# Long-convolution stage of an FFN block: filters split once into a rounded part and a remainder and loaded as two Toeplitz tiles in three slots

## The reference

```python
K = _get_kernel(log_dt, C, log_A_real, A_imag, Lq)          # (64, 1024)
y = jnp.fft.irfft(jnp.fft.rfft(u, n=n) * jnp.fft.rfft(K, n=n)[None], n=n)[..., :Lq]
y = (y + u * D[:, None]) * mask[:, None, :]
gate = qlinear(y, w_gate); up = qlinear(y, w_up)
h = jax.nn.silu(gate) * up
out = x + qlinear(h, w_down)
```

## Time and profile before

| what | value |
|---|---|
| timed runs | 1494.78 and 1500.71 us, median 1497.74 |
| span of the profiled execution, first to last instruction | 1487.8 us |
| TensorE matmul busy over the span | 1351.2 us (91%) |
| VectorE busy | 1002.7 us (67%) |
| ScalarE busy | 554.0 us (37%) |
| GpSimd busy | 489.5 us (33%) |
| moved by DMA | 139.21 MB, mean 94 GB/s |

### The profile page before, as it was taken

One profiled execution on the slowest core, in us unless ns is written; L12 is line 12 of the kernel. 1 busy time (PEld: TensorE's weight loads), 2 busy tenths in 40 slices (PEclk: granted clock), 3 DMA queues, 4 the chain that ended last, 5 costly groups with the idle time before them and its releaser, 6 DMA issues.

```text
span 1487.8 us, 23889 instructions
## 1 busy us (share of the span) xinstructions
PE 1351.2 (91%) x8030; PEld 810.5 (54%) x8126; DVE 1002.7 (67%) x1617; ACT 554.0 (37%) x882; POOL 489.5 (33%) x342
## 2 busy tenths in 40 slices
PE   2388888888899799999999999999999999999998
PEld 0377877778788444444444444444444444444443
DVE  7668788897998566665566556665566656665565
ACT  1155445555565133332333333332323323333333
POOL 2266666775777022112211212112221212112120
PEclk9999898999999899999999999999999999999999
DMA  0186677767785401211112111121112111121112
GB/s 4 28 254 209 214 228 221 226 204 226 247 265 172 140 15 36 57 49 35 35 42 56 42 35 35 49 56 35 35 35 63 42 35 35 49 55 37 35 29 71
DMA packets 44350, 139.21 MB, mean 94 GB/s; under 512 B 8396, under 2 KB 8606, under 8 KB 43038
## 3 DMA queue, kind: packets, MB, share of 16 engines
q1 hardware_dynamic: 44318, 138.79, 31.1%
HBM read 113.28 MB, written 25.49 MB: 93 GB/s over the span
## 4 chain that ended last, share of the span: by engine, by line
PE 51%; DVE 7%; issue 6%; ACT 1%; DVEq 0%; ACTq 0%
PE ps_o L1100 21%; PE ps_g L1074 14%; PE ps_u L1074 14%; DVE ps_o L1158 3%; PE ps_t L1085 3%; DVE h L1139 3%; DVE g_buf L1129 1%; ACT h_t L1207 1%; DVE res L1161 0%; DVEq L1138 0%; DVE h_max L1141 0%; DVE u_buf L1129 0%; ACT g_buf L1191 0%; DVEq L1157 0%; ACTq L1204 0%
## 5 line engine op out<-in xcount | busy, mean ns | idle before, releaser
L1236 POOL TENSOR_TENSOR h_int<-h,rounder 128x512 bf16<-128x512 f32 x186 | 186.7, 1025 | 778.7 <-ACT h L1197 778.7
L1074 PE MATMUL ps_g<-wgu,rows 128*128 128x512 bf16 (+1 forms) x1472 | 322.3, 358 | 8.2 <-PEq L377 4.9
L1074 PE MATMUL ps_u<-wgu,rows 128*128 128x512 bf16 (+1 forms) x1536 | 329.2, 357 | 0.0
L1129 DVE SCALAR_TENSOR_TENSOR g_buf<-ps_g,sx_all,wide 128x512 f32<-128x512 f32 x192 | 132.3, 689 | 286.8 <-PE ps_g L1074 286.6
L1191 ACT ACTIVATE g_buf<-g_buf 128x512 f32<-128x512 f32 x192 | 112.4, 585 | 569.9 <-DVE g_buf L1129 569.9
L1100 PE MATMUL ps_o<-wd,h_t 128*128 128x512 bf16 (+1 forms) x1376 | 312.2, 380 | 1.8 <-issue 0.2
L1100 PEld LDWEIGHTS ps_o<-wd,h_t 128*128 128x128 bf16 (+1 forms) x1408 | 134.2, 98 | 177.9 <-issue 34.4
L1074 PEld LDWEIGHTS ps_u<-wgu,rows 128*128 128x128 bf16 x1536 | 147.1, 98 | 151.6 <-issue 1.1
L1074 PEld LDWEIGHTS ps_g<-wgu,rows 128*128 128x128 bf16 x1536 | 140.0, 98 | 143.7 <-issue 13.2
L611 POOL TENSOR_TENSOR t_lo<-t_raw,t_hi 128x1024 fp32r<-128x1024 f32 x64 | 161.3, 2520 | 86.1 <-ACT t_hi L657 86.1
L1129 DVE SCALAR_TENSOR_TENSOR u_buf<-ps_u,sx_all,wide 128x512 f32<-128x512 f32 x192 | 132.6, 691 | 75.3 <-PE ps_u L1074 75.3
(11 more groups left out here) (148 smaller groups left out, 1225.3 us busy)
## 6 DMA issues: line engine op xcount, KB each, us to landing
t_raw<-k_rev SPq DMA_DIRECT2D x64, 512.0 KB, 6.1
rows<-in_x SPq DMA_DIRECT2D x64, 256.0 KB, 3.9
res<-in_x SPq DMA_DIRECT2D x64, 256.0 KB, 3.6
out_x<-res SPq DMA_DIRECT2D x64, 256.0 KB, 3.1
wide<-in_L_ffn_w_gate SPq DMA_DIRECT2D x22, 512.0 KB, 6.4
wide<-in_L_ffn_w_up SPq DMA_DIRECT2D x22, 512.0 KB, 7.3
wide<-in_L_ffn_w_down SPq DMA_DIRECT2D x8, 1376.0 KB, 6.6
xq_dram<-xq SPq DMA_DIRECT2D x32, 256.0 KB, 6.0
```

What stands on the lines that cost most here:

```text
L1074: last = pe.matmul(bank[:, 0:n], xq[:, par, c, :], wgu[:, NC - 1 - c, first + cols.start:first + cols.stop], start=(c == 0), stop=(c == NC ...
L1129: dve.scalar_tensor_tensor(out=buf[:, j % 2, 0:n], in0=bank[:, 0:n], scalar=sx, in1=s[:, cols], op0=ALU.mult, op1=ALU.mult).then_inc(gu_sc ...
L1236: pool.tensor_tensor(h_int[:, piece(j)], h[:, par, piece(j)], rounder[:].to_broadcast([P, n]), ALU.subtract).then_inc(h_int_ready, 1)
```

## The change

The filters are split in `long_filters`: ScalarE's copy out of PSUM writes the rounded part `k_hi`, VectorE subtracts it from PSUM into `k_lo`, and SP stores both, to `k_hi_rev` and `k_lo_rev` (two stores where there was one, each after its own semaphore). In stage 2 `t_raw`, `t_high` and `split_t` are gone; `load_t` is two loads of 512 KB, straight into `t_hi` and `t_lo`. The tiles have three slots: hh = 0 alternates between slots 0 and 1 by the parity of the iteration, hh = 1 always has slot 2. `load_t(i+2, 1)` waits for `conv_done` of `convolve(i+1, 1)`, `load_t(i+2, 0)` for that of `convolve(i, 0)`. The start of SP's list is in another order.

```diff
@@ long_filters, SP, VectorE, ScalarE
-            sp.dma_start(k_rev[:, L:L + P], zeros[:]).then_inc(k_stored, 16)
+            for k_rev in (k_hi_rev, k_lo_rev):
+                sp.dma_start(k_rev[:, L:L + P], zeros[:]).then_inc(k_stored, 16)
             for b in range(len(ps_k)):
-                sp.wait_ge(k_copied, b + 1)
                 first = b // 2 * HB
...
+                for done, k_rev, part in ((k_copied, k_hi_rev, k_hi), (k_split, k_lo_rev, k_lo)):
+                    sp.wait_ge(done, b + 1)
+                    heads = k_rev[2 * first + b % 2:2 * (first + HB):2, 0:L]
+                    sp.dma_start(heads.rearrange("a (q r) -> q a r", r=R),
+                                 part[:, b % 2, first:first + HB].bitcast(F32)).then_inc(k_stored, 16)
...
+            for b in range(len(ps_k)):
+                first = b // 2 * HB
+                dve.wait_ge(k_copied, b + 1)
+                dve.tensor_tensor(k_lo[:, b % 2, first:first + HB, :], ps_k[b][:],
+                                  k_hi[:, b % 2, first:first + HB, :].bitcast(F32), ALU.subtract).then_inc(k_split, 1)
...
-                act.activation(k_sb[:, b % 2, first:first + HB, :], ps_k[b][:], ACT.Copy).then_inc(k_copied, 1)
+                act.activation(k_hi[:, b % 2, first:first + HB, :], ps_k[b][:], ACT.Copy).then_inc(k_copied, 1)
@@ convolve_and_pack
-        t_raw = sb("t_raw", [P, 2, L])
-        t_hi = sb("t_hi", [P, 2, L], F32R)
-        t_lo = sb("t_lo", [P, 2, L], F32R)
+        t_hi = sb("t_hi", [P, 3, L], F32R)
+        t_lo = sb("t_lo", [P, 3, L], F32R)
...
+        def t_slot(par, hh):
+            return 2 if hh else par
...
-            def load_t(i, hh):
-                src = bass.AP(tensor=k_rev.tensor, offset=(2 * i + hh) * KROW, ap=[[1, P], [1, L]])
-                sp.dma_start(t_raw[:, hh, :], src).then_inc(t_loaded[hh], 16)
+            def load_t(i, par, hh):
+                slot = t_slot(par, hh)
+                for k_rev, part in ((k_hi_rev, t_hi), (k_lo_rev, t_lo)):
+                    src = bass.AP(tensor=k_rev.tensor, offset=(2 * i + hh) * KROW, ap=[[1, P], [1, L]])
+                    sp.dma_start(part[:, slot, :].bitcast(F32), src).then_inc(t_loaded[slot], 16)
...
-            load_t(0, 0)
             load_x(0)
-            load_t(0, 1)
-            for i in range(2):
-                for u in range(2):
-                    load_gu(i, i, u)
+            load_t(0, 0, 0)
+            load_t(0, 0, 1)
+            for g in range(2):
+                load_gu(0, 0, g)
             sp.wait_ge(x_turned, 2)
             load_x(1)
-            for hh in range(2):
-                sp.wait_ge(t_lo_done, hh + 1)
-                load_t(1, hh)
+            load_t(1, 1, 0)
+            for g in range(2):
+                load_gu(1, 1, g)
+            sp.wait_ge(conv_done, 2)
+            load_t(1, 1, 1)
...
                     sp.wait_ge(x_turned, 2 * i + 4)
                     load_x(i + 2)
-                    sp.wait_ge(t_lo_done, 2 * i + 3)
-                    load_t(i + 2, 0)
+                    sp.wait_ge(conv_done, 2 * i + 1)
+                    load_t(i + 2, par, 0)
...
                 if has(i, TILES - 2):
-                    sp.wait_ge(t_lo_done, 2 * i + 4)
-                    load_t(i + 2, 1)
+                    sp.wait_ge(conv_done, 2 * i + 4)
+                    load_t(i + 2, par, 1)
...
-            def split_t(i, hh):
-                pool.wait_ge(t_hi_done, 2 * i + hh + 1)
-                pool.tensor_tensor(t_lo[:, hh, :], t_raw[:, hh, :], t_hi[:, hh, :].bitcast(F32),
-                                   ALU.subtract).then_inc(t_lo_done, 1)
...
-            def t_high(i, hh):
-                act.wait_ge(t_loaded[hh], 16 * i + 16)
-                if not isinstance(i, int) or i >= 1:
-                    act.wait_ge(conv_done, 2 * i + hh - 1)
-                act.activation(t_hi[:, hh, :], t_raw[:, hh, :], ACT.Copy).then_inc(t_hi_done, 1)
...
-            def convolve(i, hh):
-                pe.wait_ge(t_lo_done, 2 * i + hh + 1)
+            def convolve(i, par, hh):
+                slot = t_slot(par, hh)
+                pe.wait_ge(t_loaded[slot], 32 * i + 32 if hh else 16 * i - 16 * par + 32)
```

More of the change, by code:

```diff
@@ L62, in reduce_turns, with long_filters @@
     tick(dve.tensor_scalar(phase, phase, bound, -bound, ALU.min, ALU.max))
-def long_filters(nc, d, log_dt, C, log_A_real, A_imag, D, lengths, k_rev, ident, ones, identb, rounder, mask, scratch,
+def long_filters(nc, d, log_dt, C, log_A_real, A_imag, D, lengths, k_hi_rev, k_lo_rev, ident, ones, identb, rounder, mask, scratch,
                  rows):
@@ L105, in long_filters @@
         last_one = sb("last_one", [1, R])
-        k_sb = turns[0:R]
+        k_hi = phase[0:R].bitcast(F32R)
+        k_lo = turns[0:R].bitcast(F32R)
         zeros = sb("zeros", [H, P])
@@ L131, in long_filters @@
         k_copied = sem("k_copied")
+        k_split = sem("k_split")
         k_stored = sem("k_stored")
@@ L156, in _ @@
             sp.wait_ge(consts_ready, 1)
-            sp.dma_start(k_rev[:, L:L + P], zeros[:]).then_inc(k_stored, 16)
+            for k_rev in (k_hi_rev, k_lo_rev):
+                sp.dma_start(k_rev[:, L:L + P], zeros[:]).then_inc(k_stored, 16)
             for b in range(len(ps_k)):
-                sp.wait_ge(k_copied, b + 1)
                 first = b // 2 * HB
[L161 to L164, removed]
+                for done, k_rev, part in ((k_copied, k_hi_rev, k_hi), (k_split, k_lo_rev, k_lo)):
[3 more added lines that the diff above has]
+                                 part[:, b % 2, first:first + HB].bitcast(F32)).then_inc(k_stored, 16)
+            sp.wait_ge(k_stored, 32 + 32 * len(ps_k))
         @block.vector
@@ L362, in _, with convolve_and_pack @@
                 last.then_inc(k_done, 1)
-def convolve_and_pack(nc, d, x, w_gate, w_up, w_down, k_rev, xq_dram, s_dram, ident, ones, identb, rounder, mask,
+def convolve_and_pack(nc, d, x, w_gate, w_up, w_down, k_hi_rev, k_lo_rev, xq_dram, s_dram, ident, ones, identb, rounder, mask,
                       wgu, wd, sx_all, w_f32, x_rows):
@@ L410, in convolve_and_pack @@
         ps_i = psum("ps_i", [P, P])
-        t_loaded = [sem(f"t_loaded{j}") for j in range(2)]
+        t_loaded = [sem(f"t_loaded{j}") for j in range(3)]
         x_loaded = sem("x_loaded")
@@ L627, in unround @@
                                    ALU.subtract).then_inc(w_int_ready, 1)
-            split_t(0, 0)
-            split_t(0, 1)
             unround(0, 0, 0, None)
@@ L694, in _ @@
             for hh in range(2):
-                t_high(0, hh)
                 u_high(0, hh)
@@ L707, in body @@
                 if has(i, TILES - 1):
-                    t_high(i + 1, 0)
                     u_high(i + 1, 0)
@@ L720, in body @@
                 if has(i, TILES - 1):
-                    t_high(i + 1, 1)
                     u_high(i + 1, 1)
@@ L854, in await_x @@
                 pe.wait_ge(x_loaded, 32 * i + 32)
-                pe.wait_ge(u_lo_done, 2 * i + hh - 1)
+                if not isinstance(i, int) or i >= 1:
+                    pe.wait_ge(u_lo_done, 2 * i + hh - 1)
             def turn_x(i, hh):
@@ L874, in convolve @@
                     for k, (t, u) in enumerate(parts):
-                        last = pe.matmul(out[:, dist * B:NC * B], t[:, hh, block_cols], u[:, hh, 0:n],
+                        last = pe.matmul(out[:, dist * B:NC * B], t[:, slot, block_cols], u[:, hh, 0:n],
                                          start=(dist == 0 and k == 0), stop=(dist == NC - 1 and k == 2),
@@ L917, in body @@
                 for hh in range(2):
-                    convolve(i, hh)
+                    convolve(i, par, hh)
                     if not last_one:
@@ L1250, in build @@
     d = split_dims(x.shape, w_gate.shape)
-    k_rev = nc.dram_tensor("k_rev", [d["H"], d["KROW"]], F32).ap()
+    k_hi_rev = nc.dram_tensor("k_hi_rev", [d["H"], d["KROW"]], F32).ap()
+    k_lo_rev = nc.dram_tensor("k_lo_rev", [d["H"], d["KROW"]], F32).ap()
     xq_dram = nc.dram_tensor("xq_dram", [d["TILES"], P, d["L"]], BF16).ap()
@@ L1270, in build @@
             mask = early.enter_context(nc.sbuf_tensor("mask", [P, d["C"], d["B"]], BF16))
-            long_filters(nc, d, log_dt, C, log_A_real, A_imag, D, lengths, k_rev, ident, ones, identb, rounder, mask,
+            long_filters(nc, d, log_dt, C, log_A_real, A_imag, D, lengths, k_hi_rev, k_lo_rev, ident, ones, identb, rounder, mask,
                          wide, rows)
-            convolve_and_pack(nc, d, x, w_gate, w_up, w_down, k_rev, xq_dram, s_dram, ident, ones, identb, rounder, mask,
+            convolve_and_pack(nc, d, x, w_gate, w_up, w_down, k_hi_rev, k_lo_rev, xq_dram, s_dram, ident, ones, identb, rounder, mask,
                               wgu, wd, sx_all, wide, rows)
```

8 lines of the change are left out of this document (1 added, 7 removed).

## The result

The changed kernel takes **1657.4 us** (median of 2 runs, 1657.26 to 1657.54) where the kernel before takes 1497.74: 1.108 times as long, 95% interval 1.101 to 1.115. Its profiled execution took 1657.54 us around a span of 1655.8. I had said 1614, in a range of 1550 to 1656: slower was right, and the size was 43 us short, 1.4 us beyond the range.

What follows compares the result with a forecast made beforehand. Bound: the stage 2 loop of x buffer free, load x, land, turn, second convolution. Later x adds 68.6 + 39.9 + 6.7 + 1 = 116 us to 1497.7, giving 1614 us; range 1550 to 1656.

Steps and rivals of the forecast that it cites:

- T0: Stage 2: the moment when `convolve(i, 1)` is over and `spread_inv` starts; the prediction counts x's landing from it.
- Rivals 2 and 3: Stage 2: 2, bytes hidden and x not late, 1502 us, chance 0.04; 3, faster by freed engines, 1461 us, chance 0.03.
- Rival 2: Stage 2 DMA: by capacity a gate period needs 12.3 us, the change costs about 4 us; 1502 us, chance 0.04.
- Rival 1: Stage 2: x is late but TensorE's clock stays up; 1551 us, chance 0.11.
- each further 512 KB load behind it: Burst at T0: t_lo and gate weights, behind the first load, take 1.29 us each at 406 GB/s, 2.58 us together.
- The pair of x: End of the burst at T0: the two x loads land 2.97 us behind the loads ahead of them.
- Gate part: Stage 2, 20 periods: x at T0 + 9.56, 16.5 us a period for 13.07, +68.6 us.
- Down part: Stage 2, 6 periods: `w_down` directly ahead of x, x at T0 + 11.74, 19.2 us a period, +39.9 us.
- The four periods without weights: Stage 2, bodies 20, 21, 22, 29: x at T0 + 8.27, 14.2 us each with 1.0 for the clock, +6.7 us.
- The start: End of stage 1: added subtracts and store +1 us; gain and loss of the reordered load start cancel (bounds -1 and +1).
- the 10 us that I laid around the span: Whole kernel: the timed median lies 10 us above the span of 1487.8, a distance taken as unchanged.

Runs made afterwards that it cites:

- E2: Kernel before with only the filter tile of hh = 1 issued after the end of the second convolution, no byte added; 1638.22 us.
- E11: Changed kernel with its three pairs of filter slots used in rotation, loop written out over six bodies, same bytes; 1543.5 us.
- E12: Changed kernel with rotating filter slots and a second x buffer for odd i up to 19; 1509.8 us.
- E10: Changed kernel with 19 matmuls per iteration added to fill TensorE's wait for x; 1611.7 us.
- E9: Changed kernel with a second x buffer for odd i up to 19, weights and x issued ahead of the hh = 1 filter pair; 1531.58 us.

## Why the prediction was right or wrong

*The mechanism was right.* It named the pair's issue at T0, the weights and x behind it in SP's list, and the wait before `turn_max`. E2 shows it by itself, E11 by taking it away. `y_max` is late no longer; waits for `u_lo` or for the filters did not appear. x took the time that `y_max` gave up, as said. Rivals 2 and 3 fell. Rival 2's capacity is near what E12 shows (12.83 us a gate period for its 12.3): what it left out is that the queue stands idle until T0 and then has everything at once. Rival 1, the clock staying up, fell too.

*The step that failed* is a term of the sum for x's landing, "each further 512 KB load behind it", priced at 1.29 us by the 406 GB/s of the earlier trace rows; with it the size failed, on the spans 168.0 us more where I had 116. In the gate part of the changed kernel (medians of 19 periods) t_hi lands at T0 + 4.0, as summed (0.36 + 3.65). Then t_lo lands 2.3 us behind it and the weights 2.0 behind that: 4.3 us for my 2.58. The pair of x takes 2.3 for my 2.97, so that price was too high. Together x lands at T0 + 10.5 and TensorE has it at 10.7 (mean 10.85), for my 9.56.

The price of 1.29 is not wrong everywhere: the three loads behind x in the same burst land 1.2 to 1.3 us apart, at 410 GB/s. I had given the loads ahead of x the whole rate, while the loads behind them were already moving too (2.60 MB by x's landing, for 2.10 up to x). That the loads behind cost x its time is read from these bytes; no run without them was made. The Trainium skill ("SBUF — State Buffer", section "A bandwidth-pool intuition that's wrong (but worth ruling out)") puts HBM's limit at about 358 GB/s for a core, and by that figure the load would take 1.46 us (an estimate). Both prices are too low for the loads ahead of x, and the rate behind x is above that figure.

- *Gate part:* 95.0 us for my 68.6 (356.38 - 261.42). All of the 1.3 us that each period was short is x, at T0 + 10.85 for 9.56. The stretch behind it was right, 6.97 for 4.95 + 2.0, and E10 measured 2.0 for the clock there.
- *Down part:* 51.5 for 39.9. In five of the six periods (20.6 us on the mean for my 19.2) TensorE has x at T0 + 12.8 to 13.6, 1.3 us later than my 11.7, the same error as in the gate part; the stretch behind it is 7.55 us for my 7.45. The first of the six took 23.8 us, since SP came to `load_down` only 6.2 us behind T0 (505.02); its timeline, and its wait there:
```profile
505.22 0.33 SPq L523 DMA_DIRECT2D t_hi<-k_hi_rev  x1
...
506.07 0.33 SPq L607 DMA_DIRECT2D s_dram<-s_rows  x1
...
511.27 0.37 SPq L535 DMA_DIRECT2D wide<-in_L_ffn_w_down  x1
```
```profile
SPq L509 <- DMA s_dram<-s_rows: 3.6, 1, 3.6
```
  Between the gate and the down part SP stores the scales, four small stores, and waits for them to land. Behind a wait that ends at T0 this is on the path of x. In the kernel before, the stores stood behind a wait that ends in mid-iteration, and there the first down period took 14.8 us for 11.8 to 12.7 of the others. I had listed what else the late wait holds back, and left this out.
- *The four periods without weights:* 17.4 for 6.7 (50.80 + 16.71 - 50.09). Each is 2.7 us longer than my 14.2. Of this 1.2 is x (T0 + 9.4 on the mean for 8.27), and 1.5 the stretch behind it, 7.45 for 5.95: I took 1.0 us for the clock, because the wait is shorter there, but the windows have the clock at 0.80 as elsewhere.
- *The start:* +5.8 (98.01 - 92.18) for +1. "Gain and loss cancel" was wrong: x(1) now comes behind two pairs and the first weights, 2.1 us later, and the 3.7 us that remain are the clock: from there to T0(0) TensorE needs 8.57 us at 0.60 for 4.85 at 1.00. The start of that stretch, before and then after:
```profile
87.33 0.71 PE L861 MATMUL ps_x<-ident,rows 64*128 64x64 f32 x8 [0.66 <-DMA rows<-in_x]
```
```profile
89.44 0.84 PE L855 MATMUL ps_x<-ident,rows 64*128 64x64 f32 x8 [4.20 <-DMA rows<-in_x]
```
- *End of stage 2 and stage 3:* -1.7.

Sum: 95.0 + 51.5 + 17.4 + 5.8 - 1.7 = 168.0. The measured medians differ by 159.7, 8 us less, for the most part because of the 10 us that I laid around the span and took as fixed. In all executions of both kernels and of the experiments whose span is on record, 1.7 to 1.9 us lie around it, while the kernel before takes 1486 to 1502 us from one execution to the next. So its profiled execution took about 1489.6 us (an estimate: 1487.8 + 1.8), and most of my 10 us was this scatter. The range failed where its high end took 1.29 us for each further load too: it let the first landing and the clock vary, but not this price.

## What to carry to other kernels

A load that goes straight into the operand's own slot can only start when the last reader of that slot is done, so ask what must land between that moment and the next use, and add up all of it. Count the loads issued right behind as well, since they move bytes before the one that you need is complete: ahead of x loads of 512 KB landed 2.3 and 2.0 us apart here, behind it 1.3. In an issuing queue that works in order, a wait late in the iteration holds back every load behind it: 141 us here without one byte more, while 1 MB a period more cost 27 by the copy within DRAM. Give the slots away in rotation (118 us back at the same SBUF), and put such a wait behind everything that does not need it; a second buffer behind the wait gained nothing, the same buffer ahead of it 83.

## What the runs showed of the hardware

- A burst of loads into SBUF from DRAM moved 291 to 299 GB/s at a share of 1.0 while x was in it, and 410 just behind x; a whole gate part moved 300 at 1.00 (E12) and 303 at 0.93 (E9). The start of stage 2 had 406 and 208 in two stretches. What sets the rate was not settled.
- Loads that stand behind another in the one queue move bytes before it is complete: 2.60 MB had gone when the last of the first 2.10 MB landed.
- The granted clock stood at 1.00 through 20 periods once the waits were filled with matmuls (E10), and at 0.79 without; even E12, whose waits before `turn_max` in the gate part come to at most 3.7 us, had 0.90. In the kernel before, the length of the wait alone did not decide it: behind a wait of 1.41 us the stretch to the next T0 had 0.74 once (from 176.26 us) and 1.00 another time (from 244.08).
